# A scatter loop on GpSimd that waits for eight scatters at a time

## The chip, the cores and the metric

One core of a Trainium2 chip runs the kernel. The metric is the device time of one execution in microseconds (us), taken as the median of several runs. The engines are named as in the profile: PE (TensorE matmul), PEld (its weight load), DVE (VectorE), ACT (ScalarE), POOL (GpSimd), SP (SyncE).

## What is computed

A graph network with 12500 nodes of 32 features and 412500 edges that come sorted by their target `dst`. Four layers, each a sum over edges into the target node, a residual and a normalisation:

```python
x = _layernorm(x + segment_sum(x[src], dst))
agg = segment_sum(relu(x[src] + edge_attr), dst)
x = _layernorm(x + relu(relu(((1 + eps) * x + agg) @ W1.T + b1) @ W2.T + b2))
x = _layernorm(x + segment_sum(x[src] * edge_weight[:, None], dst) @ W)
x = _layernorm(x + segment_sum((norm * gate)[:, None] * x[src], dst))   # gate: sigmoid of two dot products
```

## The kernel before

The edges are cut into NCH = 52 chunks of 7936 (128 partitions x G = 62 columns). Before the four layers a first stage, the sort, puts the edges of each chunk in the order of their source. It is a pipeline over chunks:

- SP fills the 52 tables `slot_table` in DRAM with zeros (`zero_batch`, L454, eight tables of 1617 KB at a time, one batch per chunk at first) and loads the edge attributes of a chunk into `recs` (`load_recs`, L460), in two slots that alternate. The reload of a slot is let go in four spans, by the semaphore `spent` that GpSimd raises three times in each chunk, and by the landing of all its scatters.
- PE runs, in this order in a loop of two chunks: `count_before` of the next chunk (62 matmuls at L1483, then 16 groups of matmuls at L1493 and L1494, eight to a full group, each group copied out by ACT at L1282) and then `move` of this chunk (62 matmuls at L1500, then two at L1506 behind ACT's copy at L1288). The end of a `move` raises `moved_done`.
- DVE runs `rank_chunk` (L828): it waits for the copied prefixes, multiplies, waits for `moved_done` of the chunk before (so L837 starts when that has come), and some short instructions later L855 writes `idx`, the target rows of the chunk's edges, and raises `ranked`. L858 and L860 then make the operands of this chunk's `move` and raise `moved_made`.
- GpSimd runs `scatter_chunk` (L686): it waits for `ranked` and the loaded records, makes two small copies (L693, L694), and issues 62 indirect DMAs (L702), each of which scatters 128 records of 132 bytes into rows of the chunk's `slot_table`. I call these 62 a train. Column g goes by lane g % 8; each lane has a semaphore, and before a scatter GpSimd waits until the one before it on its lane has landed, so eight may be in flight.

The later stages read the tables; the first of them reads only row tables that the sort wrote another way, and no part of GpSimd's later work meets the loop. Nothing of the indices of later chunks waits for GpSimd: `idx` holds all 52 chunks, so PE and DVE may be any number of chunks ahead of it.

Of the kernel before, what the change touches and what calls it, by code (L numbers as in the profile page):

```python
# [15 lines left out]
G = 62  # L16
# [17 lines left out]
LANES = 8  # L34
# [54 lines left out]
def build_program(nc, x, src, dst, edge_attr, edge_weight, eps, w1, b1, w2, b2, w_lin, w_src, w_tgt,  # L89
# [29 lines left out]
    with ExitStack() as ctx:  # L119
# [3 lines left out]
        def sem(name):  # L123
            return ctx.enter_context(nc.semaphore(name))
# [181 lines left out]
        scattered = [sem(f"scattered{k}") for k in range(LANES)]  # L306
# [53 lines left out]
        def tables_zeroed(j):  # L360

            return 16 + 16 * min(BATCH * (j + 1), NCH - 2)

        def landed(k, chunks, more=0):

            return 16 * (chunks * len(range(k, G, LANES)) + more)
# [299 lines left out]
        def _(pool):  # L666
# [8 lines left out]
            for tile, pattern, base, mult in (  # L675
# [7 lines left out]
            pool.affine_select(out=earlier[:, :, :], in_=earlier[:, :, :], compare_op=ALU.is_gt, fill=0.0,  # L683
                               base=0, pattern=[[1, G], [0, P]], channel_multiplier=-1).then_inc(numbered, 1)

            def scatter_chunk(c, loads):  # L686
                pool.wait_ge(ranked, c.number + 1)
                pool.wait_ge(recs_in[c.slot], 16 * (len(SPANS) + 1) * c.turn + 16 * loads)
                if c.turn == 0:
                    pool.wait_ge(slots_zeroed[c.slot], 16)  # L690
                else:
                    pool.wait_ge(slots_zeroed[0], tables_zeroed((c.number - 2) // BATCH))
                pool.tensor_copy(idx_now[:, c.slot, :], idx[:, c.number, :]).then_inc(staged, 1)  # L693
                pool.tensor_copy(recs[:, c.slot, :, D], w_now[:, c.slot, :]).then_inc(staged, 1)  # L694
                pool.wait_ge(staged, 2 * c.number + 2)
                for g in range(G):
                    lane = g % LANES
                    if c.number or g >= LANES:
                        pool.wait_ge(scattered[lane], landed(lane, c.number, g // LANES))
                    if g - (LANES - 1) in (16, 32, 48):  # L700
                        pool.sem_inc(spent, 1)
                    pool.indirect_dma_start(  # L702
                        out=slot_dram[c.number], out_offset=bass.IndirectOffsetOnAxis(ap=idx_now[:, c.slot, g:g + 1], axis=0),
                        in_=recs[:, c.slot, g, :], in_offset=None).then_inc(scattered[lane], 16)

            for number in range(NCH):
                scatter_chunk(Chunk(number // 2, number % 2), 4 if number == NCH - 1 else len(SPANS) + 1)
# [1054 lines left out]
```

## Time and profile before

| | us |
|---|---|
| median of 3 runs | 10915.58 |
| lowest, highest | 10908.93, 10919.02 |
| profiled execution, span | 10922.9 |

On the profile's page the span falls into 40 equal slices of 273 us. The first 18 or 19 are the sort: there POOL is 60% busy in nearly every slice and PE 20%. Over the whole span POOL is busy for 4171.6 us (38%), 3150.3 us of it in the 3224 scatters of L702, and DVE for 6678.2 us (61%). After the sort DVE is close to full. A row of a timeline gives the start in us, the duration, the engine, the line, the operation, and in brackets the idle time of that engine before it with what ended it.

### The profile page before, as it was taken

What the parts mean: (1) busy time and instruction counts of PE and PEld (TensorE: products, weight loads), DVE (VectorE), ACT (ScalarE), POOL (GpSimd) and SP (SyncE); (2) the same over time, 40 slices, a digit from 0 to 9 for tenths busy, and PEclk for the clock granted to TensorE, in tenths of its full rate; (3) what the DMA queues carried; (4) which work ended last, traced back from release to release, by engine and by line L of the source; (5) the groups of instructions that cost most, each with busy time, mean ns of one, the idle gap of its engine ahead of it and who ended that gap; (6) DMA issues with size and microseconds to landing.
All of it is one profiled execution on the core that took longest, in us unless ns stands there. A gap on an engine that the chain in (4) does not pass through costs nothing.

```text
span 10922.9 us, 261772 instructions
## 1 busy us (share of the span) xinstructions
PE 5973.6 (55%) x110667; PEld 5323.4 (49%) x110667; DVE 6678.2 (61%) x7417; ACT 3305.1 (30%) x4321; POOL 4171.6 (38%) x4075
## 2 busy tenths in 40 slices
PE   2222222222222222223888757777768888699998
PEld 2211111111111111113777756666658888599998
DVE  3222222122222222225999899999969999899997
ACT  1100000000000000001444345555538999600000
POOL 6666666666666666664000000000004444322221
PEclk6555555555555555556999878888879999899998
DMA  9941111111111111112444355666638888566663
GB/s 152 184 69 22 22 22 22 23 22 22 22 22 23 22 22 22 22 23 70 149 149 150 102 178 194 198 198 195 197 114 284 280 277 278 191 204 198 198 198 121
DMA packets 1202248, 1327.09 MB, mean 121 GB/s; under 512 B 658739, under 2 KB 948339, under 8 KB 1201269
## 3 DMA queue, kind: packets, MB, share of 16 engines
q1 hardware_dynamic: 846161, 753.26, 25.3%
q10 hardware_dynamic: 252322, 510.54, 14.5%
q0 software_dynamic: 103168, 54.68, 2.4%
q8 instruction: 453, 7.42, 0.3%
q14 instruction: 144, 1.18, 0.0%
HBM read 917.60 MB, written 400.43 MB: 121 GB/s over the span
## 4 chain that ended last, share of the span: by engine, by line
another core or an unknown queue 34%; DVE 24%; issue 14%; PE 9%; ACT 8%; DMA 5%; DVEq 3%; ACTq 2%; SPq 0%; POOL 0%; POOLq 0%
DVE hot_d L982 6%; ACT near_now L1390 4%; DMA source_marks<-near_now 4%; DVE hot_t L993 4%; DVE msg L1148 2%; DVE hot_d L1093 2%; DVE agg L1002 2%; PE banks L1483 2%; DVE msg L1154 2%; PE banks L1493 2%; DVEq L1009 2%; PE banks L1494 2%; DVE msg L1078 1%; DVE msg L1086 1%
## 5 line engine op out<-in xcount | busy, mean ns | idle before, releaser
L702 POOL DMA_INDIRECT slot_table<-recs,idx_now x3224 | 3150.3, 977 | 1018.8 <-issue 966.8
L713 POOL TENSOR_TENSOR msg<-msg 128x448 f32<-128x448 f32 x728 | 965.2, 1326 | 4755.8 <-DVE msg L1086 3734.6
L1590 PE MATMUL banks<-hot_d,msg 128*96 128x256 bf16 x15288 | 2152.3, 293 | 658.3 <-DVE msg L1065 425.6
L1590 PEld LDWEIGHTS banks<-hot_d,msg 128*96 128x96 bf16 x15288 | 1789.0, 130 | 811.6 <-DVE msg L1065 463.4
L837 DVE TENSOR_TENSOR moved<-hot_h,banks 128x6076 bf16<-128x6076 bf16 x52 | 172.7, 3320 | 3206.7 <-remote 3010.1
L1500 PE MATMUL banks<-moved,hot_r 128*128 128x196 bf16 x3224 | 649.6, 327 | 1590.1 <-issue 1420.9
L982 DVE TENSOR_TENSOR hot_d<-lodl,banks 128x2560 bf16<-128x2560 bf16 (+1 forms) x884 | 1485.9, 1681 | 9.7 <-remote 9.2
L1500 PEld LDWEIGHTS banks<-moved,hot_r 128*128 128x128 bf16 x3224 | 371.7, 121 | 1820.2 <-issue 1623.0
L1421 ACT CAST agg<-agg 128x3584 fp8e4<-128x3584 bf16 x364 | 1146.3, 3178 | 154.2 <-DMA target_marks<-agg 112.0
L1288 ACT CAST lodl<-banks 128x196 f32 (+1 forms) x52 | 16.7, 322 | 3569.7 <-remote 3308.5
L1506 PE MATMUL banks<-ident_bf,lodl 128*98 128x128 bf16 x104 | 23.8, 328 | 1788.7 <-ACT lodl L1288 1757.7
L1506 PEld LDWEIGHTS banks<-ident_bf,lodl 128*98 (+1 forms) x104 | 14.6, 155 | 1843.8 <-issue 1803.5
L1639 PE MATMUL banks<-x_win,agg 128*128 128x32 bf16 x30576 | 825.0, 177 | 60.8 <-DVE agg L1002 53.5
L1639 PEld LDWEIGHTS banks<-x_win,agg 128*128 128x128 bf16 x30576 | 800.3, 96 | 68.3 <-issue 63.4
L993 DVE TENSOR_TENSOR hot_t<-lo_bc,banks 128x1280 bf16<-128x1280 bf16 (+1 forms) x884 | 806.7, 913 | 26.6 <-remote 15.7
L1390 ACT CAST near_now<-hot_t 128x1792 fp8e4<-128x1792 bf16 x364 | 613.5, 1685 | 581.9 <-DMA source_marks<-near_now 444.8
L982 DVE TENSOR_TENSOR hot_d<-lodl,iota_d 128x3584 bf16<-128x3584 bf16 x364 | 733.8, 2016 | 0.0
L1359 ACT CAST msg<-banks 128x480 bf16<-128x480 f32 (+1 forms) x1040 | 522.1, 554 | 659.5 <-PE banks L1590 590.9
L1691 PE MATMUL banks<-parts,near 128*128 128x33 bf16 x15288 | 679.7, 178 | 11.5 <-DMA dl_bc<-target_marks 9.7
L1691 PEld LDWEIGHTS banks<-parts,near 128*128 128x128 fp8e4 x15288 | 675.0, 95 | 18.4 <-issue 11.8
L1694 PE MATMUL banks<-b_win,dl_bc 128*128 128x3 bf16 x10192 | 665.4, 164 | 1.1 <-issue 1.1
L1694 PEld LDWEIGHTS banks<-b_win,dl_bc 128*128 128x128 fp8e4 x10192 | 614.3, 95 | 0.4 <-issue 0.4
(186 smaller groups left out, 9263.2 us busy)
## 6 DMA issues: line engine op xcount, KB each, us to landing
lo_bc<-row_table ACTq DMA_DIRECT2D x364, 448.0 KB
dl_bc<-row_table SPq DMA_DIRECT2D x364, 448.0 KB, 5.1
target_marks<-agg SPq DMA_DIRECT2D x364, 448.0 KB, 3.5
dl_bc<-target_marks SPq DMA_DIRECT2D x364, 448.0 KB, 4.2
lo_bc<-row_table ACTq DMA_DIRECT2D x468, 320.0 KB
slot_table<-zeros SPq DMA_DIRECT2D x52, 1617.0 KB, 11.2
rec_in<-slot_table ACTq DMA_DIRECT2D x364, 231.0 KB, 2.8
source_marks<-near_now ACTq DMA_DIRECT2D x364, 224.0 KB, 2.2
```

The lines of the kernel that those rows point to most:

```text
L702: pool.indirect_dma_start(out=slot_dram[c.number], out_offset=bass.IndirectOffsetOnAxis(ap=idx_now[:, c.slot, g:g + 1], axis=0), in_=recs[ ...
L713: pool.tensor_tensor(msg3[:, n % ring, :, at + D:at + 2 * D], msg3[:, n % ring, :, at:at + D], top3[:, n % ring, :, at:at + D], ALU.subtra ...
L982: v.tensor_tensor(hot[:, blk.slot, 0:half], ids.unsqueeze(2).to_broadcast([P, half, WIN, 2]), steps.unsqueeze(1).to_broadcast([P, half, WI ...
L993: v.tensor_tensor(by_two(hot_t[:, blk.slot, 0:blk.n * P]), by_two(lo_bc[:, blk.across]), far_p.to_broadcast([P, blk.n * P // 2, 2]), ALU.i ...
L1359: s.copy(msg[:, blk.slot, 5 * j:5 * j + n, :].rearrange("p g f -> p (g f)"), banks[:, 2 * blk.slot + j, 0:3 * D * n]).then_inc(taken[0], 1)
L1390: s.copy(near_now[:, :].bitcast(F8), hot_t[:, blk.slot, :], saturate=False).then_inc(near_kept, 1)
L1421: s.copy(far_now[:, n % 2, :].bitcast(F8), hot_td[:, n % RING].rearrange("p k m -> p (k m)"), saturate=False).then_inc(far_kept, 2)
L1500: mm = t.matmul(banks[:, 5, 0:2 * HB].rearrange("p (q h) -> p q h", q=2), group_of(hot_r, g), moved[:, :, g // 2, :, g % 2], start=(g == 0 ...
L1590: mm = t.matmul(banks[0:3 * D, 6 + blk.par, 0:WIN], rows[:, g, :], hot[:, blk.slot, g // 2, :, g % 2], start=(blk.b == 0 and g == 0), stop ...
L1639: mm = t.matmul(banks[:, r % 2, D * g:D * g + D], hot_td[:, r, k, g * P:(g + 1) * P], x_win[:, r, k, q * D:(q + 1) * D], start=(k == 0 and ...
L1691: t.matmul(banks[:, blk.third, at:at + YA], near8[:, kept_of(blk, g)], parts3[:, blk.h0 + g, q, :], start=(q == 0), stop=(q == 2))
L1694: mm = t.matmul(banks[:, blk.third, at + YA:at + 36], hot_far[:, blk.b, k, slots_of(blk, g)], b_win[:, blk.par, k, 0:3], start=(k == 0), s ...
```

## The change

GpSimd no longer waits for one lane ahead of each scatter. Ahead of columns 8, 16, ..., 56 it waits on all eight lanes until everything issued so far of this chunk has landed, and it does so once more behind column 61. The first eight scatters of a chunk wait for none. `spent` is raised behind the waits at columns 16, 32 and 48 (before it was raised in the issue order at columns 23, 39 and 55, behind the wait for columns 15, 31 and 47).

```diff
+            def wait_run(c, g):
+                for lane in range(LANES):
+                    pool.wait_ge(scattered[lane], landed(lane, c.number, len(range(lane, g, LANES))))
+
             def scatter_chunk(c, loads):
...
                 for g in range(G):
                     lane = g % LANES
-                    if c.number or g >= LANES:
-                        pool.wait_ge(scattered[lane], landed(lane, c.number, g // LANES))
-                    if g - (LANES - 1) in (16, 32, 48):
+                    if g and lane == 0:
+                        wait_run(c, g)
+                    if g in (16, 32, 48):
                         pool.sem_inc(spent, 1)
                     pool.indirect_dma_start(
                         out=slot_dram[c.number], out_offset=bass.IndirectOffsetOnAxis(ap=idx_now[:, c.slot, g:g + 1], axis=0),
                         in_=recs[:, c.slot, g, :], in_offset=None).then_inc(scattered[lane], 16)
+                wait_run(c, G)
```

## Rows read from the trace of the kernel before

**Rows 1.** The page's 40 slices: busy tenths of POOL, busy share of DMA.
```profile
POOL 6666666666666666664000000000004444322221
...
DMA  9941111111111111112444355666638888566663
```

**Rows 2.** Groups by line, POOL, 1000 to 4900 us: count, busy, mean; idle before.
```profile
L702 POOL DMA_INDIRECT slot_table<-recs,idx_now x2482 | 2414.2, 973 | 755.6 <-issue 744.5 <-POOL recs L694 11.1
...
L693 POOL COPY idx_now<-idx 128x62 int32<-128x62 int32 x40 | 9.4, 235 | 705.8 <-DVE idx L855 705.8
```

**Rows 3.** Timeline of POOL, chunk 21: first and last scatter, then chunk 22's start.
```profile
2091.27 0.98 POOL L702 DMA_INDIRECT slot_table<-recs,idx_now  x1 [0.28 <-POOL recs L694]
...
2169.10 0.97 POOL L702 DMA_INDIRECT slot_table<-recs,idx_now  x1 [0.30 <-issue]
2187.76 0.24 POOL L693 COPY idx_now<-idx 128x62 int32<-128x62 int32 x1 [17.70 <-DVE idx L855]
...
2188.51 0.98 POOL L702 DMA_INDIRECT slot_table<-recs,idx_now  x1 [0.28 <-POOL recs L694]
```

**Rows 4.** Timeline of DVE around the same train.
```profile
2081.22 3.32 DVE L837 TENSOR_TENSOR moved<-hot_h,banks 128x6076 bf16<-128x6076 bf16 x1 [68.44 <-remote]
...
2090.23 0.22 DVE L855 SCALAR_TENSOR_TENSOR idx<-spot,spill 128x62 f32 x1 [0.15 <-issue]
...
2094.57 3.31 DVE L860 TENSOR_TENSOR moved<-hot_h,banks 128x6076 bf16<-128x6076 bf16 x1
...
2178.46 3.32 DVE L837 TENSOR_TENSOR moved<-hot_h,banks 128x6076 bf16<-128x6076 bf16 x1 [72.79 <-remote]
```

**Rows 5.** Timeline of PE, the first chunk's move.
```profile
77.00 7.67 PE L1500 MATMUL banks<-moved,hot_r 128*128 128x196 bf16 x62 [12.26 <-DVEq L861]
```

**Rows 6.** Timeline of ACT: copies of prefix groups, two in each of two trains.
```profile
451.33 0.60 ACT L1282 CAST before<-banks 128x392 bf16<-128x392 f32 x1 [9.91 <-remote]
459.73 0.60 ACT L1282 CAST before<-banks 128x392 bf16<-128x392 f32 x1 [7.80 <-remote]
...
629.63 0.60 ACT L1282 CAST before<-banks 128x392 bf16<-128x392 f32 x1 [17.59 <-issue]
649.99 0.60 ACT L1282 CAST before<-banks 128x392 bf16<-128x392 f32 x1 [19.75 <-issue]
```

**Rows 7.** Timeline of POOL: two idle pauses between those copies of the first train.
```profile
451.71 0.97 POOL L702 DMA_INDIRECT slot_table<-recs,idx_now  x1 [0.99 <-issue]
...
455.60 0.97 POOL L702 DMA_INDIRECT slot_table<-recs,idx_now  x1 [1.65 <-DMA slot_table<-recs,idx_now]
```

**Rows 8.** Timeline of POOL, chunk 20: first scatter, a long one, last.
```profile
1993.94 0.98 POOL L702 DMA_INDIRECT slot_table<-recs,idx_now  x1 [0.28 <-POOL recs L694]
...
2009.20 1.80 POOL L702 DMA_INDIRECT slot_table<-recs,idx_now  x1 [0.30 <-issue]
...
2072.38 0.96 POOL L702 DMA_INDIRECT slot_table<-recs,idx_now  x1 [0.30 <-issue]
```

**Rows 9.** DMA issues: KB each, median us to landing.
```profile
source_marks<-near_now ACTq DMA_DIRECT2D x364, 224.0 KB, 2.2
...
slot_weight<-w_col ACTq DMA_DIRECT2D x52, 49.0 KB, 2.0
```

**Rows 10.** Timeline of SP: the load that waits until chunk 21 has landed.
```profile
2172.74 0.70 SPq L466 DMA_DIRECT2D recs<-edge_attr  x1
```

**Rows 11.** What POOL waited for, 70 to 730 us: total us, times, longest.
```profile
POOL slot_table L702 <- issue: 130.2, 379, 1.7
POOL idx_now L693 <- DVE idx L855: 58.2, 3, 20.9
POOL slot_table L702 <- DMA slot_table<-recs,idx_now: 38.7, 53, 2.6
```

**Rows 12.** Timeline of POOL: end of chunk 0, start of chunk 1.
```profile
146.46 0.96 POOL L702 DMA_INDIRECT slot_table<-recs,idx_now  x1 [0.30 <-issue]
...
157.16 0.98 POOL L702 DMA_INDIRECT slot_table<-recs,idx_now  x1 [2.38 <-DMA slot_table<-recs,idx_now]
```

**Rows 13.** Timeline of SP: one batch of eight zero fills, merged.
```profile
355.20 58.15 SPq L449 DMA_DIRECT2D slot_table<-zeros  x8
```

## Prediction

> **What bounds the kernel now.** I began with the page's slices [rows 1]. The change touches only GpSimd's scatter loop, which fills the first 18 to 19 slices; the DMA share tells two parts of it apart: slices with 0.9 or more up to about 600 us, where SP's zero fills run, and 0.1 from about 700 us to the end of the sort. The groups by line over 1000 to 4900 us give one chunk of the quiet part [rows 2]: 40 trains of 62 scatters in 3900 us are 97.5 us for each, in which POOL sits idle 705.8 / 40 = 17.6 us until DVE's L855 has written the next chunk's rows. So POOL is not full: about a sixth of the stage is a wait for DVE.
>
> The next question is what DVE waits for. Over one period [rows 3, 4]: L837 starts at 2081.22 (it waits for the end of PE's move), L855 at 2090.23, the first scatter of chunk 21 at 2091.27, the last at 2169.10, L837 again at 2178.46, the next chunk's first scatter at 2188.51. Hence the period of 97.24 us is the sum of four legs: train, first to last scatter, 77.83; last scatter to moved, 9.36; L837 to L855, 9.0; from there to the first scatter, 1.05 (2188.51 less 2178.46, less 9.0). The middle two hang on PE: its move is let go by the end of L860 at 2097.88 and is over 80.6 us later, though the same 62 matmuls take 7.67 us in the first chunk [rows 5]. DVE is idle for 72.79 us of it. The same PE work shows two paces [rows 6]: a prefix group is eight matmuls and eight weight loads, and in a train without pauses one takes 649.99 - 629.63 = 20.36 us, which is 16 x 1.27: one PE instruction for each scatter. In an earlier train a group took 8.40 us, and in that stretch POOL had two idle pauses of 0.99 and 1.65 us in place of the usual 0.30 [rows 7]. So I read it that PE crawls while scatters are issued without a pause, and catches up in pauses and behind the train's end. The profile calls the releaser "remote" or "issue", so the coupling is an inference, not a row.
>
> **Part 1, the waits taken away.** A scatter follows the last after 0.30 us whether or not it had a lane wait (the first eight of the first chunk have none): 2482 of them have 744.5 us of "issue" idle, 0.30 each, and no row of landing [rows 2]. In the quiet part the lanes never held anything up; nothing is gained there. In the first seven trains they did: 38.7 us on landings, and 130.2 us of issue over 379 scatters, of which 0.30 each is 114, so 16 more [rows 11]. Those 55 us go, because fewer are in flight when the next is issued.
>
> **Part 2, the new pauses, quiet part.** Seven in a train, each from the start of the eighth scatter to its landing plus the restart, less the 1.27 that passes anyway. No row times a scatter's landing. Nearest rows: a 49 KB store takes 2.0 and a 224 KB store 2.2 from issue to landing [rows 9]; SP's load, which waits for the landing of the whole train, is out 3.64 after the last scatter's start [rows 3, 10], a ceiling, since SP's own issue work is in it. I take 2.0 (the small store is nearest: a scatter moves 16 KB), and 0.28 for the restart, as behind the copies [rows 3]. Pause: 2.28 - 1.27 = 1.0 us; bounds 0 (if it landed within the period) and 2.6. Seven: +7.1 us (0 to 18), train 84.9. The seven waits that are not last are passed while the last scatter is in flight. The wait behind column 61 costs about 1 us in front of the copies, hidden under the 17.6 us for as long as those last.
>
> The Trainium skill (DMA: Bandwidth & Descriptors, section on the anatomy of one DMA on the SWDGE path) puts the fixed cost of a DMA from GpSimd at about 2.0 us, most of it the write receipt; an estimate by that page would be the same 7.1 us for a train, and no row here times it.
>
> **Part 3, what PE gives back.** With PE unhelped, the leg from last scatter to moved stays 9.36 and the period grows by the full 7.1. A natural trial says otherwise: in chunk 20 one scatter took 1.80 us in place of 0.97, and the train 78.44 us in place of 77.83 [rows 8, 3], 0.6 longer; from its last scatter to L837 it took 2081.22 - 2072.38 = 8.84, 0.5 shorter. So some 5/6 came back. Applied to 7.1: 5.9 back, leg 3.4, period 84.9 + 3.4 + 10.1 = 98.4, +1.1. The first trains, which have pauses, say about the same: 7 trains in 660 us are 94.3 each, with 58.2 / 7 = 8.3 of wait for DVE [rows 11]. I keep +1.1 for the 44 quiet periods: +48 us. Bounds: PE not helped, +7.1 x 44 = +312; PE no limit at all, then POOL alone sets the pace, 84.9 + 1.0 (landing of the last) + 0.5 (copies) + 1.3 = 87.7, so -9.5 x 44 = -420.
>
> **Part 4, the pauses under the zero fills.** Here a landing takes far longer. Column 56 of chunk 0 started at 146.46; chunk 1's first scatter, which waited for it, at 157.16 [rows 12]: 10.4 us after the restart's 0.28 is taken off. Eight lanes x 1.27 = 10.2 covered that; the new wait doesn't. A loaded pause costs 10.4 + 0.28 - 1.27 = 9.4, a quiet one 1.0. One batch of fills is issued over 58 us [rows 13] and takes about 15 to 20 more to drain, and SP starts the next when a train has landed, so a train of 120 us has about 75 loaded: four pauses, counting the one at its end, and four quiet. Train to train: 62 x 1.27 = 78.7, + 1 for the copies, + 4 x 9.4 + 4 x 1.0 = 41.6, so 121; now it is 94.3. Five such trains: +134. The first train meets more load (+40), the seventh only a batch of two tables (+3). Sum +177. PE has pauses of 9 us there, so it never holds POOL up, and gets one or two chunks ahead; that pays back some 15 us when the quiet part begins. I take +162. Bounds: +60 if a landing under load is about 5 us when few are in flight, +220 if the fills stretch over more pauses.
>
> **Part 5, the rest.** `spent` comes behind the landing of columns 15, 31 and 47, as before, so SP's loads keep their place in the train, and they have 97 us of lead. The last train runs 7 us longer beside the first stage behind the sort: +7. Later stages hold no changed instruction.
>
> **Sum.** 48 + 162 + 7 = +217 on the span of 10922.9, so 11140; the median stands 7.3 under the profiled span, so 11133.
>
> **Rivals.** (a) *PE is set free.* If in each pause PE runs near its full pace (a group of 16 in 0.5 us where ACT follows it without a wait), seven pauses are enough for the remaining move, `moved_done` comes within the train, and POOL goes from train to train: 87.7. It decides once the period falls under 97.24 - 169 / 44 = 93.4. Price: -420 + 169 = -251, so 10665. For it: the 5/6 of chunk 20 is near full pace. Against: the pauses of 0.99 and 1.65 us brought only about nine extra instructions (16 in 8.4 us, against 7 at one per 1.27), and the first trains, with pauses, still waited for DVE. A pace between, 92 to 94.5, would cancel part 4.
> (b) *PE is not helped at all*, since the pauses are too short for it: +312 + 169 and the same for the rest, 11397. For it: it goes on crawling with 0.30 us pauses, and it needs 9.36 us behind a train. Against: rows 6 to 8.
> (c) *PE's move is slow by itself*, and the scatters are no cause. It then ends 80.6 us after L860 wherever the train ends, the train of 84.9 still ends before it, and the period stays at 97.24: +0 + 169, so 11085. The Trainium skill (SBUF — State Buffer, section on who interferes with whom) says that DMA never contends with a compute engine, which would give this case. Against it stand the 7.67 us of the first chunk, whose move ran beside scatters too, and the two paces.
> (d) *The change does nothing*: landings under 1.27 us in the quiet part, and the fills cheap: 10916. The 10.4 us of rows 12 speak against it.
>
> **How the numbers follow.** Chances: forecast 0.44, with its own range 10990 to 11270 (part 4's bounds, and a period of -0.5 to +3); (a) 0.20; the pace between, near no change, 0.08; (b) 0.13; (c) 0.12; (d) 0.03. Runs of this kernel tell a change of 0.2% (22 us) from none. Faster: (a) and a part of the pace between, 0.24. Within 0.2%: 0.07. Slower: the forecast, (b), (c), and what is left, 0.69. The range of 8 in 10 takes in (b) above and (c) below, and reaches down past no change to a part of (a): 10830 to 11420.
>
> **What would show it.** In the profile after: idle of POOL ahead of every eighth scatter, 1.3 us in the quiet part with "DMA" as releaser (part 2), about 9.7 during the fills (part 4); the first train of the quiet part starting at about 890 us in place of 728; period 98.4, with 3.4 from last scatter to L837 (part 3; 9.4 would be (b), 2.3 would be (c)); POOL's idle until L855 down from 17.6 to some 11. If that wait is near zero in most chunks, it is (a). If the landings under load are short, part 4 fails first; it is the largest term and rests on one pair of rows.

## The result, and the profile of the changed kernel

The kernel before took 10917.3 us (median of 4 runs, 10908.9 to 10934.9), the changed kernel 9066.7 us (4 runs, 9052.4 to 9084.2): a ratio of 0.8305, 95% interval 0.8295 to 0.8315. The profiled execution of the changed kernel has a span of 9050.7 us against 10922.9. I had forecast 11133, and my range ended at 10830. This ratio is not the whole result either: on two of seven occasions the kernel before itself took about 7330 us, and on the one of these on which the change was run it makes the kernel 16% slower (experiment 2). First the trace of the occasion on which the ratio above was taken.

Line numbers have moved: the scatter L702 is now L706, the copy L693 is L697, DVE's L837, L855 and L860 are L842, L860 and L865, and PE's move L1500 is L1505.

The page of the changed kernel, busy tenths in 40 slices (226 us each; 273 us each in rows 1):
```profile
PE   5666666466666666455455457776888885999998
...
POOL 4545666666666666666666640000444443222221
...
DMA  7785111244444443344444446663888885666663
```
POOL's scatters end in the 24th slice, at about the same time in us as before. What has changed is what runs beside them: TensorE is busy by 0.4 or more from the first slice on, and the DMA share rises from the eighth slice on, where it was 0.1 until the end of the sort in rows 1. The later stages have moved in beside the scatters.

The groups by line, POOL, 1000 to 4900 us, which answer to rows 2:
```profile
L706 POOL DMA_INDIRECT slot_table<-recs,idx_now x2479 | 2477.6, 999 | 1328.6 <-issue 893.2 <-DMA slot_table<-recs,idx_now 424.1 <-POOL recs L698 11.2
...
L697 POOL COPY idx_now<-idx 128x62 int32<-128x62 int32 x40 | 12.1, 303 | 70.8 <-issue 65.6 <-DMA slot_table<-recs,idx_now 3.6 <-DVE idx L860 1.6
```
POOL does as many scatters in this stretch as before (2479, 2482). Its idle time has changed hands: the wait for DVE's rows is 1.6 us where it was 705.8, and 424.1 us stand under the landing of scatters, where rows 2 had none.

DVE's timeline at 1516 to 1547 us, which answers to rows 4:
```profile
1516.27 3.32 DVE L842 TENSOR_TENSOR moved<-hot_h,banks 128x6076 bf16<-128x6076 bf16 x1
...
1525.28 0.22 DVE L860 SCALAR_TENSOR_TENSOR idx<-spot,spill 128x62 f32 x1 [0.15 <-issue]
...
1546.27 3.32 DVE L842 TENSOR_TENSOR moved<-hot_h,banks 128x6076 bf16<-128x6076 bf16 x1 [3.60 <-remote]
```
From one chunk's L842 to the next are 30.0 us; it was 97.24. DVE idles 3.60 us ahead of it instead of 72.79.

Where the stages end: the move's last 62 matmuls (first and last start are in the row), POOL's last scatter, and the whole of the edges stage's matmul L1623:
```profile
L1505 PE MATMUL banks<-moved,hot_r x62: 247/253/367, 1708.5 to 1715.9; 128*128 128x196 bf16 x62
...
5352.52 0.97 POOL L706 DMA_INDIRECT slot_table<-recs,idx_now  x1 [0.30 <-issue]
...
L1623 PE MATMUL banks<-parts,hot_t x15288: 176/187/232, 3708.7 to 6180.1; 128*128 128x32 bf16 x199
```
The ledger, in us of each profiled span (last start of the stage's own matmul or scatter):

| | sort | last scatter | edges | behind the edges |
|---|---|---|---|---|
| before, 10922.9 | 5024 | 5098 | 8060 | 2863 |
| changed, 9050.7 | 1716 | 5353 | 6180 | 2871 |

The scatters end 255 us later, and the whole is 1872 us shorter. All of that is the edges stage ending 1880 us earlier. Of the two stages behind the sort, the sum over sources now starts at 1755 instead of 5070 and the edges at 3709 instead of 6321: each starts when the stage ahead of it is over. In the kernel before it was the sort that kept them back and no wait for scatters; the sum over sources began at 5070, ahead of the last scatter at 5098. Of these stages only the edges wait for scatters at all, chunk by chunk: ScalarE passes `wait_scattered(act, blk.chunk + 1)` ahead of a chunk's first load.

### The profile page after: what moved, and what is told of

Same layout as the page of the kernel before. It is cut to its first block, busy times and chain, and to the rows that moved or that the text cites. A ratio compares the mean times of both kernels' runs of the same rounds, so it can differ in the third digit from the quotient of the medians.

```text
span 9050.7 us, 263229 instructions
## 1 busy us (share of the span) xinstructions
PE 6201.8 (69%) x110667; PEld 5646.6 (62%) x110667; DVE 6723.1 (74%) x7417; ACT 3318.8 (37%) x4321; POOL 4264.7 (47%) x4075
## 3 DMA queue, kind: packets, MB, share of 16 engines
q14 instruction: 155, 1.27, 0.0%
## 4 chain that ended last, share of the span: by engine, by line
DVE 24%; PE 20%; another core or an unknown queue 19%; issue 17%; ACT 10%; DMA 5%; DVEq 3%; ACTq 3%; SPq 0%; POOL 0%; POOLq 0%
DVE hot_d L987 5%; PE banks L1595 5%; ACT agg L1426 3%; PE banks L1505 3%; ACT near_now L1395 3%; DMA target_marks<-agg 2%; DVE msg L1153 2%; PE banks L1499 2%; DMA source_marks<-near_now 2%; PE banks L1498 2%; DVE msg L1159 2%; DVE hot_t L998 2%; PE banks L1488 2%; DVE hot_d L1098 2%
## 5 line engine op out<-in xcount | busy, mean ns | idle before, releaser
L706 POOL DMA_INDIRECT slot_table<-recs,idx_now x3224 | 3236.7, 1004 | 1927.6 <-issue 1135.3
L1595 PE MATMUL banks<-hot_d,msg 128*96 128x256 bf16 x15288 | 2520.2, 322 | 496.4 <-DVE msg L1070 300.3
L1595 PEld LDWEIGHTS banks<-hot_d,msg 128*96 128x96 bf16 x15288 | 2039.6, 146 | 688.9 <-DVE msg L1070 328.9
L1623 PE MATMUL banks<-parts,hot_t 128*128 128x32 bf16 x15288 | 488.3, 183 | 671.3 <-DVE hot_t L998 535.3
L1623 PEld LDWEIGHTS banks<-parts,hot_t 128*128 128x128 bf16 x15288 | 456.7, 101 | 767.1 <-issue 751.2
L1604 PE MATMUL banks<-parts,hot_t 128*128 128x96 bf16 x5096 | 391.8, 238 | 584.9 <-ACT msg L1364 535.9
L1050 DVE TENSOR_TENSOR total<-banks,rec_in 128x448 f32<-128x448 f32 x364 | 226.0, 621 | 751.6 <-remote 647.2
L1604 PEld LDWEIGHTS banks<-parts,hot_t 128*128 128x128 bf16 x5096 | 336.4, 117 | 665.7 <-issue 578.3
L1696 PE MATMUL banks<-parts,near 128*128 128x33 bf16 x15288 | 680.2, 178 | 11.5 <-DMA dl_bc<-target_marks 8.4
L1498 PE MATMUL banks<-hot_h,below 128*128 128x98 bf16 x3224 | 429.3, 240 | 342.8 <-issue 130.7
```

Source lines behind the costliest of these rows:

```text
L706: pool.indirect_dma_start(out=slot_dram[c.number], out_offset=bass.IndirectOffsetOnAxis(ap=idx_now[:, c.slot, g:g + 1], axis=0), in_=recs[ ...
L1595: mm = t.matmul(banks[0:3 * D, 6 + blk.par, 0:WIN], rows[:, g, :], hot[:, blk.slot, g // 2, :, g % 2], start=(blk.b == 0 and g == 0), stop ...
L1604: mm = t.matmul(banks[:, 2 * blk.slot + g // 5, 3 * D * (g % 5):3 * D * (g % 5 + 1)], hot_t[:, blk.slot, slots_of(blk, g)], parts[:, blk.h ...
L1623: mm = t.matmul(banks[:, blk.slot, D * g:D * g + D], hot_t[:, blk.slot, slots_of(blk, g)], parts[:, blk.h0 + g, q, :], start=(q == 0), sto ...
L1696: t.matmul(banks[:, blk.third, at:at + YA], near8[:, kept_of(blk, g)], parts3[:, blk.h0 + g, q, :], start=(q == 0), stop=(q == 2))
```

## Experiment 1: without the scatters

What there was to tell apart: theory A, scatters under way hold up the engines that wait for none of them, and gaps in their issue let these go on (A1, with the question how long a gap must be) or it takes the new waits for the landings (A2); theory B, the sort is slow for a reason of its own; and, after the first runs, theories D and E on where the hold comes from.

Session is used below for kernels that ran one after another on one chip, each beside the kernel before. There were six after the result. In four of them the kernel before took 10931 to 10975 us, as in the result; I call these held sessions. In two it took 7326 and 7331 us; these are free sessions. The changed kernel was run in one of them, and in two held ones (the result and one more). All executions of one kernel within a session agreed within 0.3% for the kernel before and within 0.7% for the others.

```diff
-                    pool.indirect_dma_start(
-                        out=slot_dram[c.number], ...
-                        in_=recs[:, c.slot, g, :], in_offset=None).then_inc(scattered[lane], 16)
+                    pool.sem_inc(scattered[lane], 16)
```


> The kernel before without its 2728 row scatters: in the place of each, GpSimd raises the lane's semaphore by the same 16, so every wait stays and nobody waits longer. The slot table then holds only the zeros filled in, so the numbers of the later stages are not those of the reference; the instructions of TensorE, VectorE and ScalarE are the same. Theory A (scatters under way hold up TensorE, VectorE and ScalarE, although none of these waits for one): the sort falls from 97 us a chunk to about 25, its last group is over by about 1450; the sum over sources takes the 1142 us and the edges the 1738 us that they take in the kernel before after the scatters, and the tail its 2863: about 7200 us in all, and that is the floor for every spacing of the scatters. Theory B (the sort is slow for a reason of its own, a chain between the engines, and the new kernel gained by its order, the later stages starting early): the sort stays over 60 us a chunk, and the whole stays over 9500.

> The kernel before without its row scatters, a second time (the slot table keeps its zeros, so the later stages compute on those); 7191 us on the chip where the kernel before took 7326, 135 us less. Beside a kernel before of 10920 to 10970: if the scatters are what holds up the other engines there (theory A), 7191 within 0.5%, with the sort over by 1340, so that they cost 3750 us there and 135 us on the other chip. If that chip is slow for something else (its clock, its memory), it stays over 8000.

The 2728 of the first expectation are the scatters of the 44 quiet chunks; the edit takes out all 3224.

Measured: 7191.0 us beside 7326.4 (free) and 7196.2 beside 10975.4 (held). The page of the second:
```profile
PE   5777777588888857777777776888888869999997
...
POOL 1000000000000000000000000444444412222221
```
The sort's last matmul is at 1337 us in both, the edges' at 4326 and 4332. So the two kinds of session differ in nothing that this program does without scatters. The scatters cost 3779 us in a held session and 135 in a free one. In the held ones the hold that I read from rows 5 and 6 is real and is caused by the scatters; that was theory A. It is no matter of the clock alone: from 1000 to 4900 us of the kernel before the granted clock is 0.57 of full speed on average, mostly the lower of its two levels (1.2 and 2.4 GHz), without scatters (400 to 1300 us) 0.85, and a chunk keeps TensorE busy for 24.4 us against 17.7, so 7 of the 73 us by which a chunk is longer. VectorE is busy for 23.2 us a chunk in both; its instructions are no longer, they start later.

## Experiment 2: the same two kernels on other occasions

> The kernel before, unchanged, run again beside the others of its call, for its trace. In the call before this one the kernel before took 7326 us where it had taken 10917 us in the comparison with the new kernel. Theory D (the hold that scatters have on TensorE, VectorE and ScalarE belongs to the chip or to how the program came to lie on it, and is there or not there for all runs of a call): it takes either 10917 or 7326 us, within 0.5%. With 7326 its trace has the sort at 24 to 25 us a chunk, over by 1340, the sum over sources in 1115 us, and the edges bound by the scatters: the last group of the edges stage ends some 50 us behind the last scatter, near 4400. With 10917 it shows the sort at 97 us a chunk again. Theory E (the time drifts between the two from execution to execution): times in between, or both within the call.

> The new kernel, unchanged, beside the kernel before. Theory D: if the kernel before takes 7326 us here, nothing is held up, the edges stage is bound by the scatters, and the seven pauses a chunk are a loss: the trains come to 52 x 96 us in place of 52 x 80, and with the pauses of about 9 us under the zero fills the last scatter is at 5150 to 5350 in place of 4400, so that the time is 8050 to 8250, slower by 10 to 13%. If the kernel before takes 10917 us, the new one takes 9067 again, ratio 0.83.

> The kernel before, unchanged, for its trace. If it takes 7320 to 7345 us: the sort over by 1340, the sum over sources by 2490, the last scatter at 7328 - 2863 - 55 = about 4410, a train without pauses in 62 x 1.275 = 79 us, the last group of the edges stage about 53 us behind the last scatter. If it takes 10910 to 10980: the sort at 97 us a chunk, as the two traces before it.

> The new kernel, unchanged, a third time. Beside a kernel before of 7326 us (nothing held up): 8050 to 8250, slower by 10 to 13%, because the edges stage is bound by the scatters and the pauses put their end from about 4400 to 5150 to 5350. Beside one of 10920 to 10970: 9040 to 9070, ratio 0.82 to 0.83.

| session | before | changed | ratio, 95% interval |
|---|---|---|---|
| the result | 10917.3 | 9066.7 | 0.8305, 0.8295 to 0.8315 |
| held | 10948.9 | 9039.6 | 0.8252, 0.8239 to 0.8266 |
| free | 7330.6 | 8511.5 | 1.1601, 1.1575 to 1.1627 |

The kernel before, traced again, took 10966.3 and 10958.8 us; both fell in a held session, so there is no trace of it from a free one. The page of the first:
```profile
PE   2221212212122121222888857767768888699998
...
POOL 5666565665656656564000000000004444322221
```
The second of these two ran on the chip on which the kernel before had taken 7326 us in an earlier session. So theory D holds in one half, all runs of a session are of one kind, and falls in the other: it is not the chip. What it is that lasts for a session I have not found.

The changed kernel in the free session:
```profile
PE   5777776888885666742222222257888886999998
...
POOL 4455666555556555566666666623444442222221
```
Its sort is over at 1338 us and the sum over sources at 2490, as without scatters. From the 19th to the 26th slice TensorE is at 0.2. What ScalarE waits for, 2600 to 5655 us, and the ends of scatters and edges:
```profile
ACT near_now L1395 <- issue: 1299.0, 36, 67.5
ACT near_now L1395 <- DMA source_marks<-near_now: 525.7, 308, 6.5
...
ACT near_now L1395 <- DMA slot_table<-recs,idx_now: 39.9, 1, 39.9
```
```profile
5601.19 0.97 POOL L706 DMA_INDIRECT slot_table<-recs,idx_now  x1 [0.30 <-issue]
```
```profile
L1623 PE MATMUL banks<-parts,hot_t x84: 176/176/177, 5647.2 to 5654.0; 128*128 128x32 bf16 x84
```
The profile puts 1299.0 us of ScalarE's idle time, up to 67.5 us at a time, under "issue", with no releaser named. From one chunk's first scatter to the next are 99 us on average in the last 19 chunks and a chunk's edges at full pace are 33 (1738 / 52); the difference, 66, is the size of the longest waits. In the code the wait ahead of a chunk's load is the one for its scatters, and the one wait of 39.9 us is put down to them by name. The edges end 53 us behind the last scatter. A free session is thus bound by POOL, and there the pauses are a plain loss. My expectation of 8050 to 8250 was too low by some 300 us. The pauses beside the later stages were longer than I had them: of POOL's waits for landings beside the sum over sources (1400 to 2490 us) those that the profile names are 257.0 us in 77, 3.3 each, against 424.1 in 206, 2.1 each, in the held session from 1000 to 4900 us.

## Experiment 3: a pause that waits for nothing

The lane waits of the kernel before stay; ahead of each eighth scatter POOL does 4, 6 or 9 small memsets of a tile of its own. Each memset kernel was run once in each session given for it.
```diff
+                    if g and lane == 0:
+                        for k in range(9):
+                            pool.wait_ge(padded, 9 * (7 * c.number + g // LANES - 1) + k)
+                            pool.memset(pad[:, :], 0.0).then_inc(padded, 1)
+                        pool.wait_ge(padded, 9 * (7 * c.number + g // LANES))
```


> The kernel before with its eight lane waits in place; ahead of each eighth scatter (seven times a chunk) GpSimd does nine small memsets, each waiting for the one before, meant to last about 2 us, as long as the pauses of the new kernel. No wait for a landing is added. Theory A1 (what frees the other engines is the pause in the issue of scatters, however it is made): the time falls like that of the new kernel, to 8900 to 9400. Theory A2 (what frees them is the wait for the landings, its change of semaphore traffic on GpSimd's queue, or that GpSimd itself stands still): the time stays at 10917 or grows by up to 44 x 14 = 620 us.

> As the kernel with the pause of nine memsets, with four: a pause of about 0.9 us, shorter than the landing of a scatter, so that some scatter is in flight all the time. Theory A1a (the others wait only while GpSimd writes out descriptors, so every pause frees them at once): over half of the gain is there, 9000 to 9900. Theory A1b (they are free only once the last scatters have landed, 2 us after they were written out): nearly nothing is gained, 10700 to 11200.

> The kernel with the pause of nine memsets (2 us by intent, seven times a chunk, the eight lane waits kept, no wait for a landing), a second time, beside the kernel before. On the chip where the kernel before took 7326 us it took 8057. If the kernel before takes 7326 here, that is repeated within 0.5%. If the kernel before takes 10920 to 10970: theory A1 (a pause in the issue of scatters lets the other engines go on, however it is made) says 8900 to 9300, as the new kernel's 9040 to 9067; theory A2 (the wait for the landings does it) says 10900 to 11600.

> The kernel with the pause of four memsets, a second time; 7640 us on the chip where the kernel before took 7326. Beside a kernel before of 10920 to 10970: if every pause in the issue lets the others go on at once (A1a), over half of the 1880 us is gained, 9000 to 9900; if they go on only when the last scatters have landed, 2 us after they were written out (A1b), it is 10700 to 11200.

> The kernel before with a pause of six memsets, about 1.5 us, ahead of each eighth scatter. Beside a kernel before of 10920 to 10970: four memsets gave 10671 and nine 9060. If the others are freed when the last scatters have landed, about 2 us after the last was written out (0.97 us of which is its own time in the row, so about 1.9 us of pause less 1.0 to 1.3), a pause of 1.5 us is long enough for most and the time is 9000 to 9500; if it needs the full 2 us, it stays over 10300. Beside 7326: about 7850, bound by the scatters.

| pause ahead of each eighth scatter | free | held | held: end of sort, last scatter, edges |
|---|---|---|---|
| none (before) | 7330 | 10917 to 10975 | 5024, 5098, 8060 |
| 4 memsets, 0.96 us | 7640 | 10671 | 4729, 4874, 7804 |
| 6 memsets, 1.45 us | | 10111 | 2909, 4821, 7242 |
| 9 memsets, 2.20 us | 8057 | 9060 | 1839, 5136, 6195 |
| wait for all eight (changed) | 8511 | 9067, 9040 | 1716, 5353, 6180 |

The memsets of three pauses, one of each kernel, and TensorE in the held sessions (4, 6, 9 memsets in this order):
```profile
2004.64 0.96 POOL L705 MEMSET pad<- 128x112 bf16 x4
```
```profile
2002.13 1.45 POOL L705 MEMSET pad<- 128x112 bf16 x6
```
```profile
2011.56 2.20 POOL L705 MEMSET pad<- 128x112 bf16 x9
```
```profile
PE   4421131232322333226888677777768888699998
```
```profile
PE   4445445444444444434786777777768888699998
```
```profile
PE   5556666645666556635544577776888885999998
```
A pause of 2.20 us without a wait for any landing gives the same time as the change (9060), so it is not the wait that frees TensorE but the gap in the issue of scatters: A1, and A2 is out. The gap has to be about 2 us long. From the end of a scatter's row to the start of the next are 1.24, 1.73 and 2.48 us with 4, 6 and 9 memsets, 1.95 to 2.07 in the changed kernel and 0.30 without a pause. The first brought 305 us of the 1915, the second 845. A scatter lands 2.6 us after its start (next experiment but one), 1.66 us after the end of its row. That is the order of size, but the gap of 1.73 us is long enough for that and brought less than half, so that the landing of the last scatter is what frees TensorE is not shown. In the free session both pauses only cost: 310 and 730 us.

## Experiment 4: how many scatters in a row

```diff
-                    if g and lane == 0:
+                    if g and g % 4 == 0:
                         wait_run(c, g)
```
16 in place of 4 in the second kernel. The held runs are one each.

> The new kernel with the wait behind every fourth scatter instead of every eighth: fifteen pauses a chunk instead of seven, of about 2 us each, 9 us while the table is filled with zeros. Theory A (each pause lets through what has been stuck): TensorE's stages, which took 33, 35 and 47 us a chunk in the new kernel against 25, 22 and 33 without scatters, lose at least half of that excess; a quiet train takes 62 x 1.27 + 15 x 2.2 = 112 us and the trains end at about 5700, near the end of the edges stage, so that the whole is 8400 to 8700. Theory C (the seven pauses are enough, what is left of the excess is contention of another kind): the stages keep their pace, 9050 to 9100, or the trains become the bound and it is slower.

> The new kernel with the wait behind every fourth scatter, a second time; 9574 us on the chip where the kernel before took 7326, its edges stage ending 53 us behind the last scatter at 6654. Beside a kernel before of 10920 to 10970: the trains take at least as long as there, the last scatter is at 6600 to 6900, and since the edges stage waits for each chunk's scatters, the whole is 9500 to 9800: slower than the new kernel, although TensorE's own stages, with twice the pauses, are over earlier: the sort by 1500 in place of 1716. If instead twice the pauses help as I first thought, 8400 to 8700.

> The new kernel with the wait behind every sixteenth scatter: three pauses and the end of the chunk instead of seven and the end. If each pause lets a fixed piece of TensorE's work through and the rest of a run is held up, the sort gets about half as much of it a train as in the new kernel, which did nearly three chunks of the sort in a train of 96 to 128: one and a half, so that it is over at about 3000, the scatters at about 5000, and the later stages are held up for longer: 9700 to 10300. If seven pauses were more than needed, 8900 to 9100. Beside a kernel before of 7326: 7600 to 7800, by the pauses alone.

Runs of four: 9574.0 us in the free session (ratio 1.3062, 1.304 to 1.3084), 9436.3 in a held one. Runs of sixteen, held: 10827.4, where I had 9700 to 10300. TensorE and POOL of run4_c, then TensorE of run16:
```profile
PE   5777757877846666322222222223688887899998
...
POOL 3344555454555444555555555553244444222221
```
```profile
PE   4330012223222223225888667777768888699998
```
With runs of four the held session looks like a free one: the sort ends at 1343 us (1337 without scatters) and the sum over sources takes 1169 us (1115). The scatters then end at 6517 and the edges at 6570, 53 us behind, as in the free session. My first expectation for it, 8400 to 8700, forgot that the edges stage waits for each chunk; written after the free session, the second was right in kind. With runs of sixteen the sort keeps pace with the trains (its end is at 4881) and 129 us are left of the gain. A pause is therefore not worth a fixed piece of work: seven of them do far more than twice what three do.

The hold can be seen building up within one run of eight. The changed kernel in the held session; POOL's first and last scatter of two runs, then ScalarE's copies of TensorE's results in the sum over sources:
```profile
2013.09 0.97 POOL L706 DMA_INDIRECT slot_table<-recs,idx_now  x1 [2.47 <-DMA slot_table<-recs,idx_now]
...
2022.02 0.97 POOL L706 DMA_INDIRECT slot_table<-recs,idx_now  x1 [0.30 <-issue]
2025.06 0.97 POOL L706 DMA_INDIRECT slot_table<-recs,idx_now  x1 [2.07 <-issue]
...
2033.98 0.97 POOL L706 DMA_INDIRECT slot_table<-recs,idx_now  x1 [0.30 <-issue]
2036.92 0.97 POOL L706 DMA_INDIRECT slot_table<-recs,idx_now  x1 [1.97 <-DMA slot_table<-recs,idx_now]
```
```profile
2016.87 0.56 ACT L1364 CAST msg<-banks 128x480 bf16<-128x480 f32 x1 [2.56 <-issue]
...
2023.88 0.56 ACT L1364 CAST msg<-banks 128x480 bf16<-128x480 f32 x1 [5.99 <-remote]
...
2028.08 0.56 ACT L1364 CAST msg<-banks 128x480 bf16<-128x480 f32 x1 [2.23 <-PE banks L1595]
...
2035.12 0.56 ACT L1364 CAST msg<-banks 128x480 bf16<-128x480 f32 x1 [6.18 <-remote]
```
After a pause ScalarE gets results for 4 to 5 us, three or four scatters long. Then it stands for 6 us and is released 1.9 and 1.1 us after the last scatter's start, inside the pause. In the free session the same line goes through a run of eight scatters, whose first and last start at 2015.25 and 2024.17, with waits of 0.6 to 1.5 us:
```profile
2016.93 0.56 ACT L1364 CAST msg<-banks 128x480 bf16<-128x480 f32 x1 [1.11 <-PE banks L1595]
...
2021.00 0.56 ACT L1364 CAST msg<-banks 128x480 bf16<-128x480 f32 x1 [1.22 <-PE banks L1595]
```

## Experiment 5: the trains alone, without the overlap

```diff
             def fast():
+                for k in range(LANES):
+                    pe.wait_ge(scattered[k], landed(k, NCH))
                 pe.wait_ge(parts_made, 1)
```


> The new kernel, but TensorE begins the sum over sources only when all scatters have landed, as it did in effect in the kernel before. Beside a kernel before of 10920 to 10970: the sort is over at 1750 again, the scatters at 5300, and sources, edges and the tail then take what they took in the kernel before, 1142 + 1738 and 2863 with some 110 between them: 11160, slower than the kernel before by 2%. Then the whole gain lies in the later stages running beside the scatters, and none of it in the trains. If the early stages were worth something by themselves it stays under 10500. Beside a kernel before of 7326: 11100 as well.

```profile
PE   5666651000000000001888857777767888699998
...
POOL 4556666666666666665000000000004444322221
```
Measured 11012.3 us beside 10956.0. TensorE stands nearly idle from the 7th to the 19th slice. The sort is over at 1722 us, the last scatter at 5189, the edges at 8148. The scatters themselves end 91 us later than in the kernel before, and the time is 56 us longer: the change did not bring the end of the scatters forward, and the whole gain lies in what runs beside them. I had expected 11160; the scatters ended earlier than in the full kernel, by 163 us against the trace of the result and 145 against the other held one. None of the later stages runs beside them here. This kernel is also the one in which my parts 1 to 4 can be read off cleanly. A quiet pause in it:
```profile
2019.04 0.97 POOL L706 DMA_INDIRECT slot_table<-recs,idx_now  x1 [0.30 <-issue]
2021.95 0.97 POOL L706 DMA_INDIRECT slot_table<-recs,idx_now  x1 [1.95 <-DMA slot_table<-recs,idx_now]
```
From start to start 2.91 us, so a landing takes 2.91 - 0.28 = 2.6 us and a pause adds 1.64 to the usual 1.27. A train is 89.5 us, and from one chunk's first scatter to the next are 93.5 us (33 chunks from 2010.2 to 5097.0).

## Experiment 6: a spacing between four and eight

```diff
-                    if g and lane == 0:
+                    if g and g % (8 if c.number < 7 else 6) == 0:
                         wait_run(c, g)
-                    if g in (16, 32, 48):
+                    if g in ((16, 32, 48) if c.number < 7 else (18, 36, 48)):
                         pool.sem_inc(spent, 1)
```
Five in place of six, and (20, 35, 50), in late5.

> The new kernel with runs of eight for chunks 0 to 6, whose pauses last about 9 us under the zero fills, and runs of six from chunk 7 on: ten pauses a chunk of about 2.2 us. Where scatters hold up the other engines, the hold was seen from about the fourth or fifth scatter of a run on, so that runs of six leave only one or two under it. The trains come to 62 x 1.27 + 10 x 2.2 + 3 = 104 us against 96, the last scatter to 5335 + 45 x 7 = about 5700, and the edges stage, no longer held up so much, ends with it: 5750 + 2870 = 8620 us, 400 below the new kernel; if the hold is as strong in runs of six as of eight, TensorE's stages end no earlier than 6180 and it stays at 9050 to 9150. Beside a kernel before of 7326 us it is bound by the scatters alone, 8500 to 8650.

> The kernel with runs of six from chunk 7 on, beside the new kernel on one chip. It took 8801 us beside a kernel before of 10956 (ratio 0.803), the last scatter at 5654, TensorE's stages over some 280 later. Beside 10920 to 10970: 8770 to 8830 again, 230 to 290 below the new kernel. Beside 7326: 8450 to 8600, 300 to 400 above the new kernel, since the scatters bound it there.

> The same with runs of five from chunk 7 on: twelve pauses a chunk in place of ten. If what is left over in the kernel with runs of six is still the hold (TensorE's stages ended 280 us behind the last scatter where the waits for the scatters alone leave 50), the trains become 4.5 us a chunk longer, the last scatter comes to 5860, the edges end with it at 5910 and the whole is 8770 to 8790: no gain, the bound has passed from the hold to the scatters. If the hold stays as strong, 8950 to 9050.

| free session | time | last scatter | edges |
|---|---|---|---|
| before | 7331 | | |
| changed | 8511 | 5601 | 5654 |
| six from chunk 7 | 8786 (1.1975, 1.1949 to 1.2001) | 5878 | 5931 |
| five from chunk 7 | 9026 | 6110 | 6163 |

Held session, six from chunk 7: 8800.9 us beside 10956.0, ratio 0.8034 (0.8009 to 0.8059), so 3% under the changed kernel's ratio of 0.8305 or 0.8252, though the two were never side by side in a held session. Its sort ends at 1624, its last scatter at 5654, its edges at 5933:
```profile
PE   5666666566666664555555555676888885999998
...
POOL 4555666656665565556655555401444442222221
```
I had expected the edges at 5750. They end 279 us behind the last scatter, so with runs of six some of the hold is left. Five could only be run in a free session, where the whole family follows one line: span = last scatter + 2918, in the changed kernel, in both spacings, in runs of four and in both kernels with memsets (2914 to 2921). By that line the kernel before ends its scatters at about 4411 there. No version beats both kernels in both kinds of session. The new spacing is the best in a held one, the kernel before in a free one.

## Why the prediction was wrong, by its own steps

**What bounds the kernel.** That the scatters hold up the sort was right for held sessions, down to its size: the edges end at 8059 with them and at 4332 without, and that is all of the difference in time. I wrote that the coupling was an inference; experiment 1 shows it. What the trace of before could not show is that it comes and goes with the session. What it does show, and I overlooked, is that a crawl of TensorE is only a part of it. The move of chunk 21 (rows 4) in the kernel before, then ScalarE's copy of its result:
```profile
2097.97 5.92 PE L1500 MATMUL banks<-moved,hot_r 128*128 128x196 bf16 x44 [4.49 <-DVEq L861]
...
2119.58 0.32 PE L1500 MATMUL banks<-moved,hot_r 128*128 128x196 bf16 x1 [1.08 <-issue]
2179.01 0.46 PE L1506 MATMUL banks<-ident_bf,lodl 128*98 128x128 bf16 x2 [59.11 <-ACT lodl L1288]
```
```profile
2178.55 0.32 ACT L1288 CAST lodl<-banks 128x196 f32 x1 [81.19 <-remote]
```
44 of the 62 matmuls go at full pace beside the scatters, the others one to three at a time, and the last starts at 2119.58. VectorE and ScalarE, which wait for nothing but its signal, start at 2178.46 and 2178.55, 58.5 us after its end and 9.3 us after the start of the last scatter. In the 40 moves from 1000 to 4900 us the last matmul ends 34 us after the start of the first (median) and the release comes after 80.5; without scatters both are 7.5. In the two other traces of the kernel before such late releases stand elsewhere in the chunk, in ScalarE's wait for the first counts (up to 144.7 us, "remote"). So what is held up is TensorE's issue and the release that the others wait for; the profile models the ends of matmuls, and whether the signal is late or the real end of the work isn't shown.

**Part 1**, no gain from the lane waits in the quiet part: confirmed by experiment 5, whose trains are longer, not shorter.

**Part 2**, the quiet pause: +1.64 us where I had 1.0 (bounds 0 to 2.6). The landing is 2.6 us from the scatter's start; I took 2.0 from a 49 KB store [rows 9]. The ceiling from SP's load was 3.64 [rows 3, 10], and half way between the two would have been nearer. The Trainium skill (DMA: Bandwidth & Descriptors, anatomy of one DMA, SWDGE path) has about 2.0 us for the fixed part; the trace has more, 2.6 in the quiet part, and POOL stood up to 11.7 us for one under the fills.

**Part 3**, what PE gives back: this step failed, and with it rival (a), which was the right mechanism with the wrong price. I took the extra instructions of two short pauses [rows 6, 7], nine in 8.4 us, for the pace that a pause allows. Those gaps were 0.99 and 1.65 us, and experiment 3 has since shown that gaps of 1.24 us free next to nothing and 1.73 less than half. The other ground, the trial of chunk 20 (a longer train, a leg shorter by 0.5 us), took the leg of 9.36 us from last scatter to moved for matmuls that were left over. It isn't: in 39 of the 40 moves it is 8.8 to 9.8 us, whether the last matmul had ended 3 or 61 us before the release. With 2 us the sort takes 30 us a chunk, and POOL waits for DVE 1.6 us in all instead of 705.8. The pace that POOL then sets is 93.5 at best (experiment 5), not 87.7: seven pauses of 1.64 make 11.5, not 7.1, and the rest is at the train's end.

**The frame of the sum.** The larger error is in no term. All terms and rivals are periods times 44: they ask when the scatters end. With the right period rival (a) would have been near zero. Experiment 5, in which TensorE has to wait for the scatters, is that case: its 44 quiet periods are 94.45 us on average against 97.31, which makes -126, the first trains cost 213, the last scatter comes 91 us later, and the time came out at +56. In the real kernel no stage behind the sort waits for them until the edges stage, and then only for its own chunk. I had the condition for it in hand: once PE is no longer bound to the train, its next stage starts when its own sort ends. Working that out, a sort over at about 1340 to 1720, 1142 for sources and 1738 for edges at full pace, with the scatters' end at about 5200 as the bound, gives an edges end of 5250 and a time near 8120. In the trace the last scatter is at 5353, which by the line of experiment 6 would be 8271; the other 780 us are the hold that runs of eight leave. Neither was in my list.

**Part 4**, the pauses under the fills: the mechanism was right, the size too small. What POOL waited for, 70 to 730 us, and the first scatters of chunk 1 and of chunk 7:
```profile
POOL slot_table L706 <- DMA slot_table<-recs,idx_now: 231.4, 32, 11.7
```
```profile
208.26 0.99 POOL L706 DMA_INDIRECT slot_table<-recs,idx_now  x1 [0.28 <-POOL recs L698]
...
965.42 0.98 POOL L706 DMA_INDIRECT slot_table<-recs,idx_now  x1 [0.53 <-POOL recs L698]
```
The longest pause is 11.7 us, the six trains between these rows are 126.2 us each (forecast 121 for five of them), and the quiet part begins at 965 instead of 728 (forecast about 890). That is +237 where I took +162, over my upper bound of +220: the sixth train cost as much as the others, for which I had 3 us, and nothing was paid back. **Part 5** did not matter.

**Rivals.** (b), PE not helped at all, is out by the sort's end at 1716; so are (c) and (d). For (c) I had the rule of the Trainium skill (SBUF — State Buffer, who interferes with whom) that DMA never contends with a compute engine. In a free session the trace agrees: the sort ends at 1338 us beside scatters and at 1337 without. In a held session the rule would have misled: 5024 against 1337, the only difference being the scatters. The rule speaks of SBUF's ports, and no run here shows whether the hold goes through them.

**Chances and range.** The 0.24 for faster was carried by (a). The range ended at 10830 because (a)'s floor was POOL's pace. The bound was the mistake: "PE no limit at all" was priced for POOL, not for PE's own later stages. In the free session slower was the way it went (1.16), but for a reason that I did not give, and that is luck: POOL sets the time there and no pause buys anything.

## What to carry to other kernels

When an edit may free an engine, follow that engine into its next stages and look for the first instruction that really waits for the one you slowed down; the price of the edit is set there, not at the end of the loop that it edits. A train of DMAs with gaps in it can be worth more than a dense one although it ends later, if others work beside it, and then length of gap and number of DMAs between gaps want a trial each. And run the baseline again on another occasion before a gain that rests on an interference is believed: here its sign depended on the occasion.

## What the runs showed of the hardware

- Row scatters issued by GpSimd every 1.27 us slowed a stage of TensorE, ScalarE and VectorE, which wait for none of them, to about a quarter of its pace (97.2 us a chunk against 24.6 without scatters), in five of seven sessions. VectorE's work a chunk stayed at 23.2 us; what grew were gaps in TensorE's issue and the time from a matmul's end to the release of those that wait for it, up to 61 us where it was 0.0 without scatters. In the other two sessions the sort was over at 1335 to 1338 us beside scatters, in six kernels with pauses (the kernel before itself has no trace from there), 1337 without.
- It is no property of the chip: one chip gave 7326 us for the kernel before in one session and 10931 in another. It did not change within any session. What sets it is open, and so is what path the engines share; the profile puts most of the stalls under "remote" or "issue".
- In a held session a gap of 1.95 to 2.5 us between the end of one scatter and the start of the next lets the others go, 1.24 us nearly does not. The hold comes back after three to four scatters; with runs of four it is nearly gone, with sixteen nearly full.
- The landing of a 128-row scatter took 2.6 us from its start in the quiet part. POOL's wait for one, where the profile names it, was 2.1 us on average in the held session, 3.3 beside the loads of the sum over sources and up to 11.7 under the zero fills.
